# Recurrent state sums of a two-branch layer, computed head by head in four column groups of TensorE

## The reference, cut to what matters

```python
q = softmax(q) / s;  k = (1 - smear) * softmax(k) + smear * k_prev;  k = k / s
attn = tril(einsum('bhid,bhjd->bhij', q, k) * mask)
norm = 1.0 / (attn.sum(axis=-1) + ATTN_EPS)
o = einsum('bhij,bhjd->bhid', attn * norm[..., None], v)
out = ln(silu(p) * o @ W_out, out_ln_w, out_ln_b)
```

## Time and profile before

| | |
|---|---|
| median of 3 runs | 2132.61 us (2131.91 to 2133.89) |
| the profiled execution's own time | 2133.59 us |
| its span, first to last instruction | 2131.8 us |
| PE busy | 1949.6 us, 91% |
| DVE busy | 1823.7 us, 86% |
| ACT busy | 1148.5 us, 54% |
| POOL busy | 935.3 us, 44% |
| mean granted clock of TensorE | 0.983 of 2.4 GHz |

### The profile page before, as it was taken

How to read it: one execution, slowest core, us unless ns; L and a number is a source line. 1 busy time by engine, 2 the same in 40 slices (tenths; PEclk the granted TensorE clock), 3 DMA queues, 4 the chain that set the end, 5 groups by cost and what they waited for, 6 DMA issues and landing times.

```text
span 2131.8 us, 48702 instructions
## 1 busy us (share of the span) xinstructions
PE 1949.6 (91%) x15282; PEld 1672.7 (78%) x15282; DVE 1823.7 (86%) x5354; ACT 1148.5 (54%) x2734; POOL 935.3 (44%) x941
## 2 busy tenths in 40 slices
PE   4889999989989999999999999899999999999997
PEld 2777878878878778787787887788788788888886
DVE  5688998998998999999899899778888888888884
ACT  2334544544553553554454454656776776676673
POOL 2444554554564465455455455323333333333331
PEclk8799999999999999999999999999999999999998
DMA  5000000000000000000000001121111111111110
GB/s 181 12 15 24 21 18 17 21 20 18 21 20 16 23 20 16 23 20 16 21 17 20 18 22 46 40 70 31 37 37 30 37 36 31 37 33 33 37 29 26
DMA packets 71792, 64.37 MB, mean 30 GB/s; under 512 B 12444, under 2 KB 64984, under 8 KB 71608
## 3 DMA queue, kind: packets, MB, share of 16 engines
q1 hardware_dynamic: 71736, 63.65, 9.9%
HBM read 38.45 MB, written 12.58 MB: 24 GB/s over the span
## 4 chain that ended last, share of the span: by engine, by line
PE 44%; DVE 34%; issue 15%; DMA 3%; ACT 1%; DVEq 1%; SPq 1%; POOL 1%; POOLq 0%; ACTq 0%
PE bank L1327 31%; PE bank L1332 7%; PE bank L1339 5%; DVE prob L942 5%; DVE prob L928 4%; DMA x_shift<-x 3%; DVE rot L1252 3%; DVE sq_sum L1198 2%; DVE qk_sum L1211 2%; DVE rot L1230 2%; DVE hid L1259 1%; DVE state L975 1%; DVE v_mix L1225 1%; DVE h_n L1160 1%; DVE h_n L1158 1%
## 5 line engine op out<-in xcount | busy, mean ns | idle before, releaser
L1327 PE MATMUL bank<-hT_n,w_s 128*128 128x128 f32 x3072 | 390.9, 279 | 0.5 <-ACT hT_n L713 0.5
L1327 PEld LDWEIGHTS bank<-hT_n,w_s 128*128 128x128 f32 x3072 | 366.1, 193 | 15.2 <-issue 10.8
L1332 PE MATMUL bank<-wqkv_s,xT 128*128 128x512 f32 x1152 | 318.8, 412 | 23.7 <-DVE xT L1106 18.5
L743 ACT ACTIVATE prob<-prob,row_min 128x256 f32<-128x256 f32 x512 | 256.1, 503 | 64.4 <-DVE row_min L928 62.0
L1332 PEld LDWEIGHTS bank<-wqkv_s,xT 128*128 128x128 f32 x1152 | 207.4, 191 | 81.7 <-DVE xT L1106 27.0
L942 DVE TENSOR_SCALAR prob<-prob,row_inv 128x256 f32<-128x256 f32 x512 | 224.4, 480 | 9.2
L928 DVE CUSTOM_DVE_ANT_0 prob<-bank,table,inv_norm 128x256 f32<-128x256 f32 x512 | 226.1, 478 | 2.0 <-issue 2.0
L635 POOL TENSOR_TENSOR rot_other<-raw,rot_t 128x256 f32<-128x256 f32 x256 | 186.7, 762 | 93.2 <-ACT raw L713 93.2
L598 POOL TENSOR_TENSOR inv_norm<-sq_clip,half_neg 128x16 f32<-128x16 f32 x64 | 188.7, 2948 | 63.6 <-DVE sq_clip L1201 63.6
L1327 PE MATMUL bank<-w_s,hid 128*128 128x256 f32 x768 | 206.5, 386 | 0.2 <-DVE hid L1259 0.2
L1339 PE MATMUL bank<-table,prob 128*128 128x128 f32 x1024 | 159.7, 279 | 42.6 <-DVE prob L942 40.4
(11 more groups left out here) (182 smaller groups left out, 4361.7 us busy)
## 6 DMA issues: line engine op xcount, KB each, us to landing
k_prev<-k_carry SPq DMA_DIRECT2D x32, 224.0 KB, 2.5
x_s<-in_L_attn_x SPq DMA_DIRECT2D x32, 128.0 KB, 2.1
rot_s<-in_rotary SPq DMA_DIRECT2D x64, 64.0 KB, 2.0
s_between_passes<-s_out SPq DMA_DIRECT2D x32, 128.0 KB, 1.7
x_between_layers<-x SPq DMA_DIRECT2D x32, 128.0 KB, 1.7
x_s<-x_between_layers SPq DMA_DIRECT2D x32, 128.0 KB, 2.0
xn<-x_between_layers SPq DMA_DIRECT2D x32, 128.0 KB, 2.1
s_out<-s_between_passes SPq DMA_DIRECT2D x32, 128.0 KB, 2.1
```

The source lines that it names most:

```text
L743: ins = act.activation(prob[:, h, :], prob[:, h, :], ACT.Exp, bias=row_min[:, c:c + 1], scale=-1.0, accum_out=row_sum[:, c:c + 1])
L1327: return pe.matmul(out, lhsT, rhs, start=first, stop=last)
L1332: ins = pe.matmul(out, halved(left[:, a]), halved(right[:, b]), start=first and n == 0, stop=last and n == 2)
```

## The change

`state_sum` is one step in place of two. Before, each of the four groups was one product: all four heads' keys (128 columns of weights) with all four heads' values (132 columns), of which only the diagonal blocks were used. Now each of the 16 heads has its own product: 32 columns of weights with 33 moving columns, and its result goes to the partitions 32r to 32r+31 and the columns 33g to 33g+32 of `mix_bank[0]`. The order of the loop goes over the four column groups r of the array within each g. All four groups' sums fit one bank (132 columns).

`state_add` is one step too: four additions of 32 partitions x 132 numbers, where there were eight of 32 x 66. Both halves stand after `norm3`. The one `state_sum` stands after `mlp_out(m, 4, 5)`, where the second half stood. wout no longer waits for the additions, since bank 1 no longer holds sums; it waits for `o1`, the read of outputs 1. The transposes of the next window's xh, which write bank 0, wait for the additions of the window before (not in the first iteration).

```diff
-            def state_add(mix, g):
+            def state_add(mix):
-                k = str(g // 2)
-                b = mix_bank[g // 2][:, 0:2 * MR * MV].rearrange("p (g c) -> p g c", g=2)
-                dve.wait_ge(mix_pe.sem, mix_pe.at("st" + k, mix))
+                b = mix_bank[0][:, 0:MG * MV].rearrange("p (g c) -> p g c", g=MG)
+                dve.wait_ge(mix_pe.sem, mix_pe.at("st", mix))
                 dve.wait_ge(mix_pool.sem, mix_pool.at("sdec", mix))
                 for r in range(MR):
                     rows, cols = slice(r * MD, (r + 1) * MD), slice(r * MV, (r + 1) * MV)
-                    ins = dve.tensor_tensor(state[rows, g:g + 2, cols], b[rows, :, cols],
-                                            state[rows, g:g + 2, cols], ALU.add)
-                ins.then_inc(mix_dve.done("st" + k), 1)
+                    ins = dve.tensor_tensor(state[rows, :, cols], b[rows, :, :], state[rows, :, cols], ALU.add)
+                ins.then_inc(mix_dve.done("st"), 1)
...
-                if mix is not None:
-                    state_add(mix, 0)
                 if nxt is not None:
                     norm3(nxt)
                 if mix is not None:
-                    state_add(mix, 2)
+                    state_add(mix)
...
-            def state_sum(mix, k):
+            def state_sum(mix):
-                pe.wait_ge(mix_dve.sem, mix_dve.at(f"o{k}", mix))
+                pe.wait_ge(mix_dve.sem, mix_dve.at("o0", mix))
                 pe.wait_ge(mix_pool.sem, mix_pool.at("kdec", mix))
-                for g in (2 * k, 2 * k + 1):
-                    at = (g % 2) * MR * MV
-                    ins = mm(mix_bank[k][:, at:at + MR * MV], k_dec[:, g * P:(g + 1) * P],
-                             v_mix[:, g * MR:(g + 1) * MR, :].rearrange("p h d -> p (h d)"), True, True)
-                ins.then_inc(mix_pe.done(f"st{k}"), 1)
+                for g in range(MG):
+                    for r in range(MR):
+                        h = g * MR + r
+                        ins = mm(mix_bank[0][r * MD:(r + 1) * MD, g * MV:(g + 1) * MV], k_dec[:, h * MD:(h + 1) * MD],
+                                 v_mix[:, h, :], True, True)
+                ins.then_inc(mix_pe.done("st"), 1)
...
                     pe.wait_ge(norm_dve.sem, norm_dve.at("xh", mix))
+                    if mix.back(1).exists():
+                        pe.wait_ge(mix_dve.sem, mix_dve.at("st", mix.back(1)))
...
-                if mix is not None:
-                    state_sum(mix, 0)
                 if m is not None:
                     mlp_out(m, 4, 5)
                 if mix is not None:
-                    state_sum(mix, 1)
+                    state_sum(mix)
...
                     pe.wait_ge(mix_act.sem, mix_act.at("gt", mix))
-                    pe.wait_ge(mix_dve.sem, mix_dve.at("st0", mix))
-                    pe.wait_ge(mix_dve.sem, mix_dve.at("st1", mix))
+                    pe.wait_ge(mix_dve.sem, mix_dve.at("o1", mix))
```

More of the change, by code:

```diff
@@ L310, in build @@
         score_bank = [mix_bank[0], mix_bank[1], att_bank[0], att_bank[2]]
-        mix_pe = Steps(sem("mix_pe"), "xt q k v p qt kt s0 s1 s2 s3 o0 o1 st0 st1 gt wout")
+        mix_pe = Steps(sem("mix_pe"), "xt q k v p qt kt s0 s1 s2 s3 o0 o1 st gt wout")
         mix_act = Steps(sem("mix_act"), "xt exp tanh qt kt gt")
         mix_dve = Steps(sem("mix_dve"), "xl q k max p sum kinv kw qeps v kadd "
-                        "s0 s1 s2 s3 den0 rec0 o0 go0 den1 rec1 o1 go1 st0 st1 "
+                        "s0 s1 s2 s3 den0 rec0 o0 go0 den1 rec1 o1 go1 st "
                         "ystat yaggr yvar")
@@ L1639, in body @@
                     if mix.back(1).exists():
-                        pe.wait_ge(mix_dve.sem, mix_dve.at("st1", mix.back(1)))
+                        pe.wait_ge(mix_dve.sem, mix_dve.at("st", mix.back(1)))
                     pe.wait_ge(mix_dve.sem, mix_dve.at("s3", mix))
```

## The result

The changed kernel takes 2148.23 us (median of 4 runs, 2146.6 to 2149.54), the kernel before in the same job 2132.68 (4 runs, 2131.91 to 2133.89). The ratio is 1.0072, 95% interval 1.0055 to 1.0089: 15.5 us slower, where 23.6 us faster was forecast. The profiled execution took 2146.6 us.

A forecast was written before the change was run, and what follows sets the result against it. The bound was taken to be PE and DVE's hand-overs at each iteration's end. A gain of 0.70 + 0.90 - B = 0.78 us, times 31, is 24.2 us, giving 2109 us; range 2103 to 2123.

The forecast's parts named there:

- the slower one: Rival: PE's column groups run one after another in the sums; 2198 us; chance 0.07, shared with any other loss.
- 0.70 + 0.90 - 0.82: Gain per iteration: PE's idle time before wout, plus the two old sum blocks, less the new block; 0.78 us.
- B: Time the new block of sums puts between `mlp_out(m, 4, 5)` and the go transposes on PE; 0.82 us, from 0.61 to 1.20.
- Rounds: In the sums on PE, four heads in four column groups make a round; 8 rounds, 7 distances of 0.06 us.
- the first rival: Each of the 32 sum instructions on PE pays a floor of 0.029 us per start; gain 12 us, 2120 us; chance 0.20.
- serial groups: The sums' four column groups run one after another on PE, 3.5 us in all; 2198 us; chance 0.07 with other losses.
- Additions: Four DVE state additions take 1.20 us, 0.66 less than eight; counted at nothing, since DVE idles before the key halving.
- The wait: PE stands idle before wout for the state additions; removing this wait is worth 0.70 us an iteration.
- 31 times: The wait before wout came 31 times over the span; 0.78 us each gives 24.2 us.

The follow-up runs named there:

- e4: The changed kernel with 35 one-column DVE memsets ahead of the loop, but wout waits for the state additions again; 2111.8 us, ratio 0.9903.
- e1: The changed kernel with 35 one-column DVE memsets added ahead of all units; 2112.21 us, ratio 0.9906 to the kernel before.
- e10: The e1 kernel with the sums ordered group by group in unit 0 alone, alternating in all others; 2107.26 us, ratio 0.9889.
- e2: The kernel before with 30 one-column DVE memsets added ahead of all units; 2170.98 us, ratio 1.0185.

## Why the prediction was wrong

The step that failed is: "So a wout that starts earlier by x shortens the iteration by x, as long as nothing else is late there", with its later half, "all of that work is tied to the iteration's start". I followed semaphores and engines, and took for granted that DVE has its instructions when it is free. The change took six of them out of each unit of the loop, moved the loop's start by 20, and so took the loop out of what DVE holds. My sentence on the additions, "I count this at nothing", priced twelve fewer instructions a round by their busy time alone. Twelve jumps at 3.0 us (36.0 / 12) turned a gain of 20 us into a loss of 15.5. None of the rivals had this cause: the slower one was about column groups. What I wrote would make the prediction wrong, a new wait ahead of the first halving of the next iteration while DVE's wait for `stats_y` shrinks, is nearly what came. But I had tied it to the keys and not to the loop, and had it in every iteration and of the same size: the wait shrank by 0.64 us, and the new one is 2.86 us at every second iteration.

Point by point, the rest:

- **The end of an iteration.** The gain was forecast as 0.70 + 0.90 - 0.82 = 0.78 us and is 0.80 (40.47 to 39.67). That the two agree so well is in part luck, since two terms are off by 0.11 in opposite ways. The first is B: `mlp_out`'s last product starts at 655.57 + 0.81 - 0.38 = 656.00 (0.38 is one record's length), and in its stream the next would start 0.21 later ((0.81 - 0.38) / 2), at 656.21; the go transposes start at 656.92, so the block puts 0.71 between them, and this is the floor that `go1` sets: it ends at 656.38 + 0.49 = 656.87. I had 0.82. The second is the wait: from the go transposes to wout it was 651.61 - 649.60 = 2.01 us and is 658.34 - 656.92 = 1.42, which is 0.59 less and not 0.70. The key transposes start 0.93 behind the go transposes for 0.87 before, and wout 0.49 behind the key transposes for the 0.44 that I reckoned.
- **Rounds.** 0.0085 us a record is 0.034 a round, near the lower bound of 0.03 and not the 0.06 that I took. The error is hidden under `go1`. A floor of 0.029 or 25 ns a start, the first rival, is refuted, and so are serial groups.
- **Additions.** Forecast 4 x 0.30 = 1.20 us, measured 1.20; the idle time behind them, 0.86 us, is there as well.
- **The wait.** "With the sums at their old price the removed wait is worth 0.70 us": 0.59 us of it was there, but not by the removed wait alone. e4 keeps the wait and loses nothing. What removes the idle time is that the additions are over before wout could start, or that it doesn't wait for them.
- **31 times.** Measured with the loop loaded, e1 is 20.4 us under before. Both iterations of a pair gain 0.80: 40.47 to 39.67, and 40.76 to 39.97. In the two traces the thirty later iterations gain 23.3 us together, and iteration 1 gives back 3.0 (53.11 for 50.07), which I had not looked for. With the loop kept loaded the forecast of 2109 stands against 2112.2 in e1. That e10 comes to 2107.3 doesn't confirm it, since e10 has a gain at the start that the forecast didn't have.

## What to carry to other kernels

An edit that adds or removes instructions ahead of or inside a loop can move the loop to a place where it no longer stays loaded: compare the packets of the instruction queues before and after, and look at the first instruction behind the jump for idle time released by "issue". If it is there, try some idle instructions ahead of the loop before you judge the edit itself; here they turned +0.7% into -0.9%. And where a wait and a cheaper producer are changed together, either may be what opens the path: put each back alone before you credit one.

## What the runs showed of the hardware

- A loop of 348 DVE instructions costs nothing at its jump or 3.0 us (36.0 / 12), by its place alone. It was cured by 35 instructions ahead of it, spoiled again by 70, and cured by 163.
- A stall of PE can be paid again in clock, and need not be: in e2, after 2.85 us without work, six products took 2.93 us at one jump and 1.67 at another, and the iterations 44.81 and 43.25. Near the start, 0.89 us idle for 0.17 goes with 3.63 us for eight products in place of 2.07.
- Float32 matmul records of 32 weight columns and 33 moving columns start 0.0085 us apart when neighbours are in different column groups, and 0.023 apart when they share one.
- DVE additions of 32x66 whose partitions start where the last one's did follow 0.136 us after it; others 0.235.
